# The norm behind two attention stages, done group by group inside the attention's loop

## The chip, the cores and the metric

One core of one Trainium2 chip runs the whole program. The time is that of the device, in microseconds (us), from the start of an execution to its end. The core has five engines with a queue of instructions each, which run in order and wait for each other by semaphores: PE multiplies matrices, DVE and POOL work on elements, ACT evaluates functions, and SP starts transfers. SBUF holds the data, and PE writes into eight banks of PSUM.

## What is computed

Four layers run over x of shape (16, 256, 128), that is 4096 tokens of 128 values. Each layer has an attention-like part and a feed-forward part, and each of the eight parts looks like this:

```python
h = _layernorm(x, axis=-1) * (1 + ca) + sa
x = x + ga * attention(h)
h = _layernorm(x, axis=-1) * (1 + cb) + sb
x = x + gb * feed_forward(h)
```

The scales and shifts differ for each of the 16 batches of 256 tokens. Two of the attention parts have 16 heads of 8 values: that of layer 1, which is causal and goes through a latent of 32, and that of layer 3, which sees all of a batch's 256 tokens. Behind the first comes a soft mixture of experts, whose first step needs the normed tokens of all batches. Behind the second comes a choice of 512 tokens for each of 8 experts. It begins with the logits: the normed tokens times an 8-column matrix.

## The kernel before

x stays in SBUF as `k.X`, 32 tiles of 128 tokens. The normed, scaled and shifted h of a part stands in `k.HT`, turned so that its columns are tokens. A norm over all tokens (`layernorm_dve`, `layernorm_pe`, `layernorm_act`, L283 to L317) goes as follows. The variance of each tile is known from `stats` (L179, L181). DVE adds eps to all 32 variances, ACT takes the square root, DVE the reciprocal. Then for each tile DVE subtracts and scales (L294) into one of eight tiles `xn`, PE turns that into a quarter of a PSUM bank (L170), and ACT scales and shifts a batch's two tiles into `k.HT` (L317). In the last layer PE also computes the logits there (`logits_pe`, L1188), a few for every two tiles turned.

A second form works on a group of four tiles, 512 tokens or two batches, numbered 0 to 7: `group_root_dve` (L328) takes the root by three rounds of Newton's method, all on DVE and on 4 columns: 6 instructions in the first of its three parts, 4 in the second and 4 in the third, each waiting for the one before. `group_rows_dve` (L348) norms two tiles, `group_turn_pe` turns four, `group_out_act` (L365) writes the two batches. The norm ahead of each attention with 16 heads has this form already. Its groups 0 to 6 run inside the loop of the part before, and its last one, group 7, runs in slots 0 to 5 of the attention (steps `norm` and `ht`).

An attention with 16 heads (`heads_*`) is a list of steps that `heads_steps` writes out by slot, and each engine walks the whole list in order. There are 4 slots for each batch, 64 in all, and a few behind them. In a slot, `far` (PE, then ACT's exponential L1085) makes the scores of one slot, `near0` and `near1` (PE L883, then DVE L1003 and L1005 or L1008) find the maximum of a slot six ahead, and `pv` applies the weights of the slot before. The rest of a batch's work is spread by the slot number modulo 4, as `misc` has it: `q0` and `k0` in 0, `out`, `nat0` and `nat1` in 1, `mb` at the start of 2 and `mt`, `q1` and `k1` behind it, `v`, `back` and `x` in 3. `x` adds the result of a batch to `k.X`, 11 slots after the batch's first, and `stats` of that batch come a slot later. All small products share two banks, `a.side`, in turn: a use waits until the use before last has been read out (`heads_room`).

The program does the parts one after the other: `heads_*`, then `layernorm_*`, then the mixture (`soft_*`) or the choice (`gate_rows_pe`, `pick_*`).

Of the kernel before, what the change touches and what calls it, by code (L numbers as in the profile page):

```python
# [324 lines left out]
ROOTS = 3  # L325
# [30 lines left out]
def group_turn_pe(k, n, e, B, bank):  # L356
    for j in range(4):
        e.wait_ge(*k.s_xn(32 * n.no + 4 * B + j + 1))
        transpose(k, e, bank[:, 128 * j:128 * j + 128], n.xn[(4 * B + j) % 8]).then_inc(k.s_turned.sem, 1)
# [384 lines left out]
AHEAD_UNITS = 9  # L744


def heads_plan(k, l, no, causal, w, t_w, norm):
    a = K()
    a.l, a.no, a.causal, a.w, a.t_w, a.norm = l, no, causal, w, t_w, norm
    a.scale = 8 ** -0.5  # L750
    a.slots = 4 * NB
    a.w1 = 128 if causal else 256
    a.qT, a.kT = ([k.QK[:, 512 * i + 2560 * j:512 * i + 2560 * j + 512] for i in range(5)] for j in range(2))
    R, G = Region(k.T, TW), Region(k.gbbc, 2048)
    a.PT = R.many(2, 2048)
    a.oT, a.va = R.many(2, 1024), R.many(2, 1024)
    a.whole, a.mb, a.junk = R.many(2, 512), R.many(2, 256), [k.W2[:, 384 * i:384 * i + 384] for i in range(2)]
    a.mx, a.rin = R.many(2, 32), R.many(2, 16)
    a.pick, a.hb = R.get(256).bitcast(BF16), R.get(16).bitcast(BF16)
    a.wo, a.msel, a.rows = R.get(128), R.get(4), [R.many(2, 32) for _ in range(2)]  # L760
    a.bga = R.get(16)
    a.mT = [R.get(128).bitcast(BF16) for _ in range(2)]
    a.lats, a.oN, a.oc, a.yT = G.many(2, 256), G.many(2, 256), G.many(2, 256), G.many(2, 256)
    a.near, a.side, a.far = k.bank[0:2], k.bank[2:4], k.bank[4:8]
    a.steps = list(heads_steps(a))
    a.ahead = a.steps.index(("far", 0))
    a.uses = {}
    for step in a.steps:
        if step[0] not in ("far", "near0", "near1", "mb", "norm", "stats"):
            a.uses[step] = len(a.uses)  # L770
    n = len(a.uses)
    a.s = sems(k, "h", side=n, free0=(n + 1) // 2, free1=n // 2, far=4 * a.slots, near=4 * a.slots, max=4 * a.slots,
               exp=4 * a.slots, kept=a.slots, high=0 if causal else 4 * NB, low=4 * NB, mb=NB, ready=5)
    return a
# [7 lines left out]
def heads_rest(a):  # L782
    return a.steps[a.ahead:]


def heads_steps(a):


    misc = {0: (("q0", 8), ("k0", 8), ("stats", -12)), 1: (("out", -9), ("nat0", -5), ("nat1", -5)),
            2: (("mt", 2), ("q1", 6), ("k1", 6)), 3: (("v", 1), ("back", -7), ("x", -11), ("lat", 9))}  # L790
    yield "wo", 0
    for s in range(-9, a.slots + 9):
        if 0 <= s < a.slots:
            yield "far", s
        if s % 4 == 2 and 0 <= s + 2 < a.slots:
            yield "mb", (s + 2) // 4
        if 0 <= s + 6 < a.slots:
            yield "near0", s + 6
        if 0 <= s - 1 < a.slots:
            yield "pv", s - 1  # L800
        if 0 <= s < ROOTS + 2:
            yield "norm", s
        if s == ROOTS + 2:
            yield "ht", 7
        for i, (step, ahead) in enumerate(misc[s % 4]):
            if i == 1 and 0 <= s + 6 < a.slots:
                yield "near1", s + 6
            n = (s + ahead) // 4
            if 0 <= n < NB and (step != "lat" or a.causal):
                yield step, n  # L810


def head(c, g):
# [24 lines left out]
    return a.s["free1" if u % 2 else "free0"](u // 2 + 1)  # L838


def heads_pe(k, a, e, steps):
    s, w = a.s, a.w
    e.wait_ge(*a.t_w)
    for step, n in steps:
        if step in ("mb", "stats", "norm"):
            pass
        elif step == "ht":
            group_turn_pe(k, a.norm, e, n, heads_room(a, e, step, n))
            e.wait_ge(*k.s_turned(32 * a.no + 4 * n + 4))
            e.nop().then_inc(s["side"].sem, 1)  # L850
        elif step == "far":
            b, c = divmod(n, 4)
            q, kk, m, at = *heads_part(a, n), a.mT[b % 2], 256 * (c % 2)
# [18 lines left out]
        elif step in ("near0", "near1"):  # L872
            b, c = divmod(n, 4)
# [107 lines left out]
def heads_dve(k, a, e, steps):  # L981
# [3 lines left out]
    for step, n in steps:  # L985
        if step == "norm":
# [83 lines left out]
def heads_act(k, a, e, steps):  # L1070
# [1 line left out]
    filled = lambda step, n: s["side"](a.uses[step, n] + 1)  # L1072
    e.wait_ge(*a.t_w)
    for step, n in steps:
        if step == "ht":
            o, free = heads_filled(a, e, step, n)
            group_out_act(k, a.norm, e, n, o)
            e.wait_ge(*k.s_h(16 * a.no + 2 * n + 2))
            e.nop().then_inc(free.sem, 1)
        elif step == "far":  # L1080
            if n >= 2:
# [1715 lines left out]
def program(nc, dram, out, phases):  # L2797
    ctx = ExitStack()
    with ctx:
# [5 lines left out]
        ln = [None] * 8  # L2805
        ln[0] = layernorm_plan(k, 0, 0, 0, r(), 0)
        a0 = attention_plan(k, 0, 0, views(k.W1, L0A), d["l0a"])
        r1 = r()
        g0 = gate_rows_plan(k, 0, 0)
        ln[1] = layernorm_plan(k, 0, 1, 1, r1, 1)  # L2810
        f0 = fold_plan(k, 0, 1, g0, d["l0f"], r1)
        ln[2] = f0.norm = layernorm_plan(k, 1, 0, 2, f0.big)
        a1 = f0.after = heads_plan(k, 1, 2, True, dict(sm, wo=sm["wproj"], bo=sm["bproj"]), d["sm"], ln[2])
        a1.begin, a1.emptied, a1.unread = f0.s["lifted"](60), (f0.s["sum"](8), k.s_h(16 * 2 + 14)), ()
        ln[3] = layernorm_plan(k, 1, 1, 3, r(), 2)
        f1 = soft_plan(k, 3, d["l1f"], d["l0f"])
        ln[4] = layernorm_plan(k, 2, 0, 4, r(), 3)
        f2 = rwkv_plan(k, 4, sm, d["sm"], d["l1f"], d["l0f"])
        r1 = r()
        g2 = gate_rows_plan(k, 2, 1)  # L2820
        ln[5] = layernorm_plan(k, 2, 1, 5, r1, 4)
        f3 = moe_plan(k, 2, 5, g2, d["l2f"], r1)
        ln[6] = f3.norm = layernorm_plan(k, 3, 0, 6, f3.big)
        a3 = f3.after = heads_plan(k, 3, 6, False, dict(sm, wo=sm["o3"], bo=sm["bo3"]), d["sm"], ln[6])
        a3.begin, a3.emptied = f3.s["lifted"](116), (f3.s["sum"](8 * 17), k.s_h(16 * 6 + 14))
        a3.unread, a3.added = range(28, 32), f3.s["tox"](8)
        r1 = r()
        g3 = gate_rows_plan(k, 3, 2)
        ln[7] = layernorm_plan(k, 3, 1, 7, r1, 5)
        f4 = pick_plan(k, 3, 7, g3, d["l3f"], r1)  # L2830
        done_by = lambda sub: k.s_aggr(32 * (sub + 1))

        block = ctx.enter_context(nc.Block())
# [32 lines left out]
        @block.tensor  # L2866
        def _(e):
            modulation_pe(k, mod, e)
            layernorm_pe(k, ln[0], e)
            attention_pe(k, a0, e)  # L2870
            layernorm_pe(k, ln[1], e, logits_pe(k, f0, e))
            gate_rows_pe(k, g0, e)
            fold_pe(k, f0, e)
            heads_pe(k, a1, e, heads_rest(a1))
            layernorm_pe(k, ln[3], e)
            soft_pe(k, f1, e)
            layernorm_pe(k, ln[4], e)
            rwkv_pe(k, f2, e)
            layernorm_pe(k, ln[5], e, logits_pe(k, f3, e))
            gate_rows_pe(k, g2, e)  # L2880
            moe_pe(k, f3, e)
            heads_pe(k, a3, e, heads_rest(a3))
            layernorm_pe(k, ln[7], e, logits_pe(k, f4, e))
            gate_rows_pe(k, g3, e)
            pick_pe(k, f4, e)

        @block.vector
        def _(e):
            modulation_dve(k, mod, e)
            e.wait_ge(*d["x"])  # L2890
            for i in range(NT):
                stats(k, e, i)
            layernorm_dve(k, ln[0], e, k.s_mod(1))
            attention_dve(k, a0, e)
            layernorm_dve(k, ln[1], e)
            fold_dve(k, f0, e)
            heads_dve(k, a1, e, heads_rest(a1))
            layernorm_dve(k, ln[3], e)
            soft_dve(k, f1, e)
            layernorm_dve(k, ln[4], e)  # L2900
            rwkv_dve(k, f2, e)
            layernorm_dve(k, ln[5], e)
            moe_dve(k, f3, e)
            heads_dve(k, a3, e, heads_rest(a3))
            layernorm_dve(k, ln[7], e)
            pick_dve(k, f4, e)

        @block.scalar
        def _(e):
            modulation_act(k, mod, e)  # L2910
            layernorm_act(k, ln[0], e)
            attention_act(k, a0, e)
            layernorm_act(k, ln[1], e)
            fold_act(k, f0, e)
            heads_act(k, a1, e, heads_rest(a1))
            layernorm_act(k, ln[3], e)
            soft_act(k, f1, e)
            layernorm_act(k, ln[4], e)
            rwkv_act(k, f2, e)
            layernorm_act(k, ln[5], e)  # L2920
            moe_act(k, f3, e)
            heads_act(k, a3, e, heads_rest(a3))
            layernorm_act(k, ln[7], e)
            pick_act(k, f4, e)

        @block.gpsimd
# [156 lines left out]
```

## Time and profile before

| what | us |
|---|---|
| median of 3 runs | 4153.87 |
| lowest and highest of them | 4150.37, 4159.74 |
| the profiled execution | 4153.31 |
| its span in the trace | 4151.6 |
| PE, DVE, ACT, POOL busy | 3767.8, 3238.5, 2228.8, 1281.9 |

The trace gives for each instruction when it ran, and how long its engine sat idle before it and for whom. "Busy" is an average over the whole span; the two stages that the change touches lie at about 1866 to 2174 us (layer 1) and 3567 to 3912 us (layer 3). A granted clock (PEclk) of 1.00 is the 2.4 GHz level of PE, 0.50 the 1.2 GHz level.

### The profile page before, as it was taken

The page shows a single profiled execution, that of the slowest core. Times are in us where ns is not written, and L with a number is a line of the kernel's source. Part 1 is how long each engine was busy: PE and PEld are TensorE (multiplying, and loading weights), DVE is VectorE, ACT ScalarE, POOL GpSimd, SP SyncE. Part 2 cuts the span into 40 slices and gives each one's busy share as a digit, 9 for nine tenths or more (in the row PEclk, how much of TensorE's full clock was granted, in tenths as well). Part 3 has the DMA queues.
Part 4 walks back from the last instruction along what each step waited for, and adds up shares of the span by engine and source line. Part 5 has one row for each costly group of instructions (what it writes and reads, how often), then busy time and mean ns, then how long its engine had stood idle before and what let it go on. Part 6 is the DMA issues. An engine that isn't in the chain of part 4 may idle for free.

```text
span 4151.6 us, 77967 instructions
## 1 busy us (share of the span) xinstructions
PE 3767.8 (91%) x25067; PEld 2529.9 (61%) x25067; DVE 3238.5 (78%) x11883; ACT 2228.8 (54%) x6889; POOL 1281.9 (31%) x1084
## 2 busy tenths in 40 slices
PE   6999999999999998989989978989978999899735
PEld 5777777777777776666654434335555666555533
DVE  6888888888888886667769986777886778788561
ACT  4877777778777774226764433332223222577401
POOL 1333333333333331014537865540000000222007
PEclk9999999999999998998999999999977999899757
DMA  2000000000000001211000000000000000000203
GB/s 121 2 1 2 1 2 1 2 1 2 2 2 2 2 1 51 88 55 62 2 2 0 0 10 1 1 0 1 1 1 32 1 1 1 31 2 2 62 9 52
DMA packets 30835, 63.57 MB, mean 15 GB/s; under 512 B 3424, under 2 KB 19808, under 8 KB 29152
## 3 DMA queue, kind: packets, MB, share of 16 engines
q1 hardware_dynamic: 24288, 52.29, 3.6%
q0 software_dynamic: 6144, 6.30, 0.9%
q8 instruction: 205, 3.36, 0.3%
q14 instruction: 198, 1.62, 0.1%
HBM read 49.93 MB, written 8.65 MB: 14 GB/s over the span
## 4 chain that ended last, share of the span: by engine, by line
PE 71%; DVE 15%; issue 7%; ACT 5%; POOL 2%; DMA 1%; DVEq 0%; POOLq 0%; ACTq 0%; SPq 0%
PE ps L462 9%; PE ps L501 9%; PE ps L170 8%; PE ps L443 6%; PE ps L486 5%; PE ps L1573 3%; PE ps L1544 3%; PE ps L1542 3%; DVE gbbc L2189 2%; PE ps L2137 2%; PE ps L2150 2%; PE ps L919 2%; DVE gbbc L2178 2%; DVE gbbc L2184 2%; PE ps L897 2%
## 5 line engine op out<-in xcount | busy, mean ns | idle before, releaser
L587 DVE CUSTOM_DVE_ANT_0 T<-ps,C 128x128 f32<-128x128 f32 x2048 | 451.4, 286 | 1.9
L734 POOL TENSOR_TENSOR W<-W,T 128x512 f32<-128x512 f32 x256 | 260.7, 1039 | 525.3 <-DVE T L623 525.3
L681 ACT ACTIVATE W<-T 128x128 f32<-128x128 f32 x1024 | 396.0, 391 | 46.0 <-DVE T L608 46.0
L734 POOL TENSOR_TENSOR T<-T 128x512 f32<-128x512 f32 x256 | 260.8, 1039 | 484.9 <-DVE T L623 484.9
L462 PE MATMUL ps<-T 64*128 64x128 f32 (+1 forms) x4096 | 405.5, 338 | 4.3 <-DVE T L587 4.3
L462 PEld LDWEIGHTS ps<-T 64*128 64x128 f32 x4096 | 344.6, 187 | 85.6 <-issue 64.5
L681 ACT ACTIVATE T<-T 128x128 f32<-128x128 f32 x1024 | 396.2, 391 | 0.0
L501 PE MATMUL ps<-W,gbbc 128*64 128x256 f32 x3072 | 388.1, 388 | 3.1 <-ACT T L698 3.1
L598 DVE COPY_PREDICATED W<-gbbc,ps 128x512 f32<-128x512 int32 x512 | 342.7, 721 | 38.0 <-PE ps L170 38.0
L170 PE MATMUL ps<-C,T 128*128 128x128 f32 (+1 forms) x1617 | 264.1, 301 | 63.4 <-DVE T L294 33.5
L170 PEld LDWEIGHTS ps<-C,T 128*128 128x128 f32 (+1 forms) x1617 | 196.0, 149 | 141.1 <-issue 45.5
L443 PE MATMUL ps<-HT,W 128*128 128x256 f32 x1024 | 278.2, 394 | 2.1 <-ACT HT L317 1.1
L1146 POOL TENSOR_TENSOR QK<-T,QK 128x512 fp32r<-128x512 f32 x128 | 162.7, 1280 | 378.3 <-ACT T L1106 260.4
L1085 ACT ACTIVATE T<-ps 128x384 f32<-128x384 f32 (+1 forms) x512 | 236.0, 550 | 71.2 <-PE ps L870 71.1
L501 PEld LDWEIGHTS ps<-W,gbbc 128*64 128x64 f32 x3072 | 197.9, 136 | 108.8 <-ACT T L698 4.2
L486 PE MATMUL ps<-T,W 128*128 128x256 f32 x1024 | 242.3, 379 | 0.8 <-ACT T L698 0.8
L575 DVE COPY_PREDICATED ps<-C,ps 128x256 f32<-128x256 int32 x512 | 195.6, 422 | 56.0 <-PE ps L462 55.8
L690 ACT ACTIVATE W<-ps 128x512 f32<-128x512 f32 x256 | 152.8, 597 | 139.0 <-PE ps L170 134.8
L1594 ACT ACTIVATE T<-ps,W 128x512 f32<-128x512 f32 x128 | 87.8, 687 | 240.2 <-PE ps L1542 240.1
L170 PE MATMUL ps<-C,W 128*128 128x128 f32 x1232 | 174.5, 284 | 45.8 <-DVE W L2762 21.2
L443 PEld LDWEIGHTS ps<-HT,W 128*128 128x128 f32 x1024 | 174.7, 190 | 64.6 <-issue 47.5
L170 PEld LDWEIGHTS ps<-C,W 128*128 128x128 f32 x1232 | 143.4, 145 | 103.1 <-issue 37.5
(403 smaller groups left out, 8801.2 us busy)
## 6 DMA issues: line engine op xcount, KB each, us to landing
T<-crow_dram SPq DMA_DIRECT2D x128, 128.0 KB, 3.0
W<-in_l1f_dram SPq DMA_DIRECT2D x1, 6152.0 KB, 18.3
W<-in_l0a_dram SPq DMA_DIRECT2D x1, 5172.5 KB, 24.7
W<-in_l2f_dram SPq DMA_DIRECT2D x1, 3160.0 KB, 11.2
W<-in_l3f_dram SPq DMA_DIRECT2D x1, 3076.0 KB, 10.9
W<-in_sm_dram SPq DMA_DIRECT2D x1, 2729.0 KB, 10.3
W<-in_l0f_dram SPq DMA_DIRECT2D x1, 2256.0 KB, 29.4
X<-in_x_dram SPq DMA_DIRECT2D x1, 2048.0 KB, 12.9
```

The costliest lines, as they stand in the source:

```text
L170: return e.transpose(out, in_, k.C["ident"])
L443: done(e.matmul(a.side[:, 256 * c:256 * c + 256], w["wq"][:, 512 * g + 128 * (2 * j + c):512 * g + 128 * (2 * j + c) + 128], x, start=True ...
L462: m = e.matmul(o, q[r, 256 * c + 128 * qt:256 * c + 128 * qt + 128], kt[r, k0:k0 + w_], start=True, stop=True)
L486: done(e.matmul(a.acc[:, 0:256], w["wo"][:, (g * a.CH + c) * 128:(g * a.CH + c + 1) * 128], a.oT[n % 2][:, 256 * c:256 * c + 256], start=( ...
L501: done(e.matmul(a.Ob[64 * r:64 * r + 64, at:at + 256], v[:, 128 * tile + g0:128 * tile + g0 + 64], x[:, r], start=(c != 1), stop=(c != 0)) ...
L575: e.copy_predicated(tiles[:, 0], old.bitcast(I32), tiles[:, 1]).then_inc(s["merged"].sem, 1)
L587: done(e.tensor_tensor_reduce(sm[:, at:at + 128], src, m, 1.0, -3.0e38, ALU.add, ALU.max, mx[:, col:col + 1]), s["masked"], x == (3 if ban ...
L598: e.copy_predicated(a.PT[t % 2][:, 512 * j:512 * j + 512].rearrange("p (h w) -> p h w", h=4), is_.unsqueeze(1).broadcast_to([P, 4, 128]).b ...
L681: done(e.activation(a.Pr[i % 4][:, at:at + w_], a.Sm[i % 2][:, at:at + w_], ACT.Exp, bias=a.ngs[i % 4][:, c:c + 1], scale=a.scale, accum_o ...
L734: e.tensor_tensor(pr, pr, a.rins[i % 4][:, c:c + 4].unsqueeze(2).broadcast_to([P, 4, 128]), ALU.mult).then_inc(s["norm"].sem, 1)
L1085: e.activation(a.PT[n % 2][:, 512 * g:512 * g + 256 + a.w1], a.far[g][:, 0:256 + a.w1], ACT.Exp, bias=0.0, scale=a.scale).then_inc(s["exp" ...
L1146: e.tensor_tensor(dst, a.whole[m % 2], dst.bitcast(F32), ALU.subtract).then_inc(s["low"].sem, 1)
```

## The change

Both norms behind the attentions with 16 heads take the form by groups, and their steps stand in the attention's own list. With B the number of a group, its three root parts stand at the end of slots 17, 18 and 19 + 8B, its two pairs of rows at the end of slots 20 and 21 + 8B, and the turning and writing, `ht2`, at the end of slot 22 + 8B. `ht2` takes a turn in the two side banks like the other small products. Slots now run to 78. So the `layernorm_*` calls behind the attentions are gone, with their root on ACT. In layer 3 the logits of batches 0 to 13 stand in slot 73, and those of batches 14 and 15 at the end. The tiles `xn` of these norms move into a free part of `k.W2`.

```diff
@@ heads_plan
-        if step[0] not in ("far", "near0", "near1", "mb", "norm", "stats"):
+        if step[0] not in ("far", "near0", "near1", "mb", "norm", "stats", "root", "rows", "logits"):
             a.uses[step] = len(a.uses)
@@ heads_steps
-    for s in range(-9, a.slots + 9):
+    for s in range(-9, a.slots + 15):
...
             n = (s + ahead) // 4
             if 0 <= n < NB and (step != "lat" or a.causal):
                 yield step, n
+        B, part = divmod(s - 17, 8)
+        if 0 <= B < 8:
+            if part < ROOTS:
+                yield "root", 8 * B + part
+            elif part < ROOTS + 2:
+                yield "rows", 8 * B + part - ROOTS
+            elif part == ROOTS + 2:
+                yield "ht2", B
+        if s == a.slots + 9:
+            yield "logits", 0
+    yield "logits", 1
@@ heads_pe
-        elif step == "ht":
-            group_turn_pe(k, a.norm, e, n, heads_room(a, e, step, n))
-            e.wait_ge(*k.s_turned(32 * a.no + 4 * n + 4))
+        elif step in ("ht", "ht2"):
+            norm = a.norm if step == "ht" else a.next
+            group_turn_pe(k, norm, e, n, heads_room(a, e, step, n))
+            e.wait_ge(*k.s_turned(32 * norm.no + 4 * n + 4))
             e.nop().then_inc(s["side"].sem, 1)
+        elif step == "logits":
+            for b in (range(14, 16) if n else range(14)) if logits is not None else ():
+                logits(b)
@@ heads_dve
+        elif step == "root":
+            group_root_dve(k, a.next, e, *divmod(n, 8))
+        elif step == "rows":
+            group_rows_dve(k, a.next, e, n // 8, ((0, 1), (2, 3))[n % 8])
@@ heads_act
-        if step == "ht":
+        if step in ("ht", "ht2"):
+            norm = a.norm if step == "ht" else a.next
             o, free = heads_filled(a, e, step, n)
-            group_out_act(k, a.norm, e, n, o)
-            e.wait_ge(*k.s_h(16 * a.no + 2 * n + 2))
+            group_out_act(k, norm, e, n, o)
+            e.wait_ge(*k.s_h(16 * norm.no + 2 * n + 2))
             e.nop().then_inc(free.sem, 1)
@@ program, PE's queue (DVE's and ACT's lose the same layernorm calls)
             heads_pe(k, a1, e, heads_rest(a1))
-            layernorm_pe(k, ln[3], e)
             soft_pe(k, f1, e)
...
-            heads_pe(k, a3, e, heads_rest(a3))
-            layernorm_pe(k, ln[7], e, logits_pe(k, f4, e))
+            heads_pe(k, a3, e, heads_rest(a3), logits_pe(k, f4, e))
             gate_rows_pe(k, g3, e)
```

On DVE, in layer 1 at the end of slot 17 (a slot that is 1 modulo 8), the changed kernel has these rows between `nat1` (L1074, L1076) and `mb` (L1044 to L1048):

```order
L1074 RECIPROCAL T<-ps 128x16
L1076 TENSOR_TENSOR gbbc<-ps,T 128x128
L334 TENSOR_SCALAR rs<-MV 128x4
L336 TENSOR_SCALAR rs<-rs 128x4
L338 TENSOR_TENSOR rs<-rs 128x4
L340 TENSOR_TENSOR rs<-rs 128x4
L342 TENSOR_SCALAR rs<-rs 128x4
L344 TENSOR_TENSOR rs<-rs 128x4
L1044 CAST T<-T 128x32
L1046 CAST T<-T 128x8x4
L1048 TENSOR_TENSOR T<-T 128x8x4
```

Before, `mb` followed `nat1` at once, and the six rows L334 to L344 were not there.

On PE, in the same stage at the end of a slot that is 6 modulo 8, the changed kernel has the four turns of `ht2` between `q1` and `k1` (L936) and the next slot's `far` (L883, L887), `near0` (L900) and `pv` (L914):

```order
L936 MATMUL ps<-gbbc,W 128x256 x4
L170 MATMUL ps<-C,W 128x128 x4
L883 MATMUL ps<-QK 128x256 x4
L887 MATMUL ps<-T 128x256 x4
```

Before, `far` followed `k1` at once. The nop that PE carries out behind the turns, when they are done, is not among the rows.

On PE, at the end of layer 3's attention, the changed kernel has `out` of batch 15 (L969), then `ht2` of group 6, the last `x`, the logits of 14 batches (L1210), `ht2` of group 7, and the last logits ahead of the gate's rows (L257):

```order
L969 MATMUL ps<-gbbc,T 128x256
L170 MATMUL ps<-C,W 128x128 x4
L170 MATMUL ps<-C,gbbc 128x128 x2
L1210 MATMUL ps<-W,HT 128x8 x28
L170 MATMUL ps<-C,W 128x128 x4
L1210 MATMUL ps<-W,HT 128x8 x4
L257 MATMUL ps<-C,modT 128x128 x16
```

Before, 32 turns with 32 logits among them stood between the last `x` and L257, and nothing stood between `out` and the last `x`.

## Rows read from the trace of the kernel before

**Rows 1.** Windows: length, then PE, PEld, DVE, ACT, POOL busy, then PEclk.
```profile
2066.00:2083.80 17.80, 16.91 (x200) 11.11 (x198) 13.66 (x83) 12.75 (x29) 9.44 (x9) 1.00 0.01 2
3812.19:3851.07 38.88, 36.66 (x395) 23.00 (x394) 33.74 (x77) 28.48 (x56) 10.13 (x9) 1.00 0.01 2
...
2160.00:2165.00 5.00, 1.50 (x6) 0.74 (x6) 3.53 (x15) 2.08 (x3) 0.00 (x0) 0.68 0.00 0
...
3894.00:3902.00 8.00, 8.00 (x43) 7.92 (x43) 5.58 (x21) 4.16 (x9) 0.00 (x0) 0.50 0.60 172
```

**Rows 2.** Chain of waits, layer 1: start, length, engine and line.
```profile
2091.53 0.68 PE ps L913 x4
...
2103.31 0.18 DVE T L1023
...
2105.11 0.49 PE ps L883 x3
```

**Rows 3.** Chain of waits, layer 3.
```profile
3827.14 1.20 DVE T L1008 x2
...
3831.11 0.61 ACT T L1106
```

**Rows 4.** Timeline of DVE, group 7 of the norm ahead of layer 3's attention.
```profile
3571.94 0.17 DVE L334 TENSOR_SCALAR rs<-MV 128x4 f32<-128x4 f32 x1
...
3573.14 0.69 DVE L1015 TENSOR_TENSOR T<-ps,W 128x512 f32<-128x512 f32 x1
...
3578.15 0.22 DVE L338 TENSOR_TENSOR rs<-rs 128x4 f32<-128x4 f32 x1
...
3579.00 1.29 DVE L1008 TENSOR_REDUCE T<-ps 128x2 f32<-128x512 f32 x2
...
3595.58 0.59 DVE L352 TENSOR_SCALAR W<-X,MV,rs 128x128 f32<-128x128 f32 x2
```

**Rows 5.** Timeline of DVE in both loops: in brackets the idle time before.
```profile
2090.60 0.29 DVE L1003 CUSTOM_DVE_ANT_0 W<-ps,C 128x128 f32<-128x128 f32 x1 [1.69 <-PE ps L883]
...
3834.55 1.29 DVE L1008 TENSOR_REDUCE T<-ps 128x2 f32<-128x512 f32 x2 [0.73 <-PE ps L883]
```

**Rows 6.** Timeline of ACT, layer 3: exponentials of a batch's first slots, and L365.
```profile
3593.01 2.06 ACT L1085 ACTIVATE T<-ps 128x512 f32<-128x512 f32 x4 [0.78 <-PE ps L870]
...
3602.02 1.04 ACT L365 ACTIVATE HT<-ps,modT 128x256 f32<-128x256 f32 x2
...
3614.00 2.06 ACT L1085 ACTIVATE T<-ps 128x512 f32<-128x512 f32 x4 [0.51 <-PE ps L870]
...
3815.00 2.06 ACT L1085 ACTIVATE T<-ps 128x512 f32<-128x512 f32 x4 [0.51 <-PE ps L870]
...
3834.44 2.06 ACT L1085 ACTIVATE T<-ps 128x512 f32<-128x512 f32 x4 [0.51 <-PE ps L870]
```

**Rows 7.** Timelines of POOL and of DVE at one place in layer 1's attention.
```profile
1888.86 1.10 POOL L1150 TENSOR_SCALAR_AFFINE_SELECT T<-T 128x1024 f32<-128x1024 f32 x1 [0.24 <-ACT T L1085]
...
1889.25 1.04 DVE L352 TENSOR_SCALAR W<-X,MV,rs 128x128 f32<-128x128 f32 x2
```

**Rows 8.** Chain of waits, end of layer 1's attention and of the norm behind it.
```profile
2158.31 0.27 DVE T L1053
...
2161.83 0.43 DVE X L1063
...
2173.88 3.73 PE ps L170 x32
```

**Rows 9.** Timeline of ACT at the same place.
```profile
2161.25 1.28 ACT L313 ACT_TABLE_LOAD   x1
```

**Rows 10.** Chain of waits, end of layer 3's attention and of the norm behind it.
```profile
3889.12 0.43 DVE X L1063
...
3907.47 4.07 PE ps L1188 x20
3911.54 5.99 PE ps L257 x32
```

More of the change, by code:

```diff
@@ L744, with heads_plan @@
 AHEAD_UNITS = 9
-def heads_plan(k, l, no, causal, w, t_w, norm):
+def heads_plan(k, l, no, causal, w, t_w, norm, after):
     a = K()
-    a.l, a.no, a.causal, a.w, a.t_w, a.norm = l, no, causal, w, t_w, norm
+    a.l, a.no, a.causal, a.w, a.t_w, a.norm, a.next = l, no, causal, w, t_w, norm, after
     a.scale = 8 ** -0.5
@@ L838, in heads_taken, with heads_pe @@
     return a.s["free1" if u % 2 else "free0"](u // 2 + 1)
-def heads_pe(k, a, e, steps):
+def heads_pe(k, a, e, steps, logits=None):
     s, w = a.s, a.w
@@ L844, in heads_pe @@
     for step, n in steps:
-        if step in ("mb", "stats", "norm"):
+        if step in ("mb", "stats", "norm", "root", "rows"):
             pass
-        elif step == "ht":
-            group_turn_pe(k, a.norm, e, n, heads_room(a, e, step, n))
-            e.wait_ge(*k.s_turned(32 * a.no + 4 * n + 4))
+        elif step in ("ht", "ht2"):
+            norm = a.norm if step == "ht" else a.next
+            group_turn_pe(k, norm, e, n, heads_room(a, e, step, n))
+            e.wait_ge(*k.s_turned(32 * norm.no + 4 * n + 4))
             e.nop().then_inc(s["side"].sem, 1)
+        elif step == "logits":
+            for b in (range(14, 16) if n else range(14)) if logits is not None else ():
+                logits(b)
         elif step == "far":
@@ L2807, in program @@
         a0 = attention_plan(k, 0, 0, views(k.W1, L0A), d["l0a"])
+        spare = lambda: Region(k.W2[:, 768:], 1024)
         r1 = r()
@@ L2812, in program @@
         ln[2] = f0.norm = layernorm_plan(k, 1, 0, 2, f0.big)
-        a1 = f0.after = heads_plan(k, 1, 2, True, dict(sm, wo=sm["wproj"], bo=sm["bproj"]), d["sm"], ln[2])
+        ln[3] = layernorm_plan(k, 1, 1, 3, spare())
+        a1 = f0.after = heads_plan(k, 1, 2, True, dict(sm, wo=sm["wproj"], bo=sm["bproj"]), d["sm"], ln[2],
+                                  ln[3])
         a1.begin, a1.emptied, a1.unread = f0.s["lifted"](60), (f0.s["sum"](8), k.s_h(16 * 2 + 14)), ()
-        ln[3] = layernorm_plan(k, 1, 1, 3, r(), 2)
         f1 = soft_plan(k, 3, d["l1f"], d["l0f"])
-        ln[4] = layernorm_plan(k, 2, 0, 4, r(), 3)
+        ln[4] = layernorm_plan(k, 2, 0, 4, r(), 2)
         f2 = rwkv_plan(k, 4, sm, d["sm"], d["l1f"], d["l0f"])
@@ L2820, in program @@
         g2 = gate_rows_plan(k, 2, 1)
-        ln[5] = layernorm_plan(k, 2, 1, 5, r1, 4)
+        ln[5] = layernorm_plan(k, 2, 1, 5, r1, 3)
         f3 = moe_plan(k, 2, 5, g2, d["l2f"], r1)
         ln[6] = f3.norm = layernorm_plan(k, 3, 0, 6, f3.big)
-        a3 = f3.after = heads_plan(k, 3, 6, False, dict(sm, wo=sm["o3"], bo=sm["bo3"]), d["sm"], ln[6])
+        ln[7] = layernorm_plan(k, 3, 1, 7, spare())
+        a3 = f3.after = heads_plan(k, 3, 6, False, dict(sm, wo=sm["o3"], bo=sm["bo3"]), d["sm"], ln[6],
+                                  ln[7])
         a3.begin, a3.emptied = f3.s["lifted"](116), (f3.s["sum"](8 * 17), k.s_h(16 * 6 + 14))
         a3.unread, a3.added = range(28, 32), f3.s["tox"](8)
-        r1 = r()
         g3 = gate_rows_plan(k, 3, 2)
-        ln[7] = layernorm_plan(k, 3, 1, 7, r1, 5)
-        f4 = pick_plan(k, 3, 7, g3, d["l3f"], r1)
+        f4 = pick_plan(k, 3, 7, g3, d["l3f"], r())
         done_by = lambda sub: k.s_aggr(32 * (sub + 1))
@@ L2897, in _ @@
             heads_dve(k, a1, e, heads_rest(a1))
-            layernorm_dve(k, ln[3], e)
             soft_dve(k, f1, e)
@@ L2904, in _ @@
             heads_dve(k, a3, e, heads_rest(a3))
-            layernorm_dve(k, ln[7], e)
             pick_dve(k, f4, e)
@@ L2915, in _ @@
             heads_act(k, a1, e, heads_rest(a1))
-            layernorm_act(k, ln[3], e)
             soft_act(k, f1, e)
@@ L2922, in _ @@
             heads_act(k, a3, e, heads_rest(a3))
-            layernorm_act(k, ln[7], e)
             pick_act(k, f4, e)
```

## The prediction

> **What bounds the kernel now.** I looked at the windows of the two attentions first, for how full each engine is. In layer 1 a batch takes 17.80 us, PE works in 16.91 of them and DVE in 13.66; in layer 3 two batches take 38.88 us, with PE at 36.66 and DVE at 33.74 [rows 1]. So DVE is free for 4.1 us per batch in layer 1 and for (38.88 - 33.74) / 2 = 2.6 us in layer 3. That looks like room. But all queues run in order, so next I read the chain of waits, to see whose work has no slack. In layer 1 the chain lies on DVE from `near1` through `nat0`, `nat1` and `mb` (L1023 at 2103.31) to the next `near0`, and PE's `near1` (L883, 2105.11) waits for it; later in the batch it runs through ACT's `q1` and `k1` to PE's `v` (L913 at 2091.53) [rows 2]. In layer 3 it runs through DVE's `near1` (L1008 at 3827.14) and then through ACT's `k1` (L1106 at 3831.11) [rows 3]. DVE's free time lies elsewhere: 1.69 us behind slot 2 modulo 4 in layer 1, 0.73 us behind slot 3 modulo 4 in layer 3 [rows 5].
>
> Last the two ends. In layer 1 the last `x` is added at 2161.83 and the mixture's first turns start at 2173.88, 12.05 us later [rows 8]. In layer 3 the last `x` stands at 3889.12 and the gate's rows at 3911.54, 22.42 us later [rows 10]. In that end PE is busy in 8.00 of 8.00 us at a granted clock of 0.50 [rows 1], and the last 20 logit matmuls take 4.07 us, 0.204 us each [rows 10]. A logit is carried out as two matmuls, so there are 64 of these for 32 tiles.
>
> **What a group adds in the loop.** Prices come from group 7 of the norm ahead [rows 4]. The first root part runs from 3571.94 to 3573.14, 1.20 us. The second runs from 3578.15 to 3579.00, 0.85 us; the third is as long. A pair of rows takes 0.59 us. L365 for two batches takes 1.04 us on ACT [rows 6]. Group by group, at each place:
> - First root part, behind `nat1` and ahead of `mb`: nothing covers it. In layer 1 `mb` and PE's `near1` are on the chain [rows 2], so 1.20 us. In layer 3 PE and DVE are level there, within about 0.15 us, so 1.05 us. PE, and then everybody, waits.
> - Second and third part: in layer 1 the 1.69 us of free time covers the second [rows 5]; the third meets a similar gap. In layer 3 the third falls into 0.73 us [rows 5] and the second ahead of a stretch in which the chain is on ACT. I take 0. If that cover is gone, each costs 0.85 us.
> - First pair of rows, behind `stats`: it delays `near0`, and PE's `near1` is only partly waiting. 0.3 us in layer 1, 0.2 us in layer 3.
> - Second pair, behind `nat1` like the first root part: 0.6 us in layer 1, 0.45 in layer 3.
> - `ht2`, behind `k1`: on ACT it stands between `k1` and the next exponentials, 1.04 us and some 0.15 for the wait for its own writes. On PE four turns and the wait for their end come ahead of `far`. `v` now takes the side bank that `ht2` held, so PE waits at `v` for ACT's `ht2`; queued behind are `near1`, `back` and `x`. Both ways it is about 1.2 us, on the chain in both layers [rows 2, 3].
>
> The sum is 1.20 + 0.3 + 0.6 + 1.2 = 3.3 us in layer 1 and 1.05 + 0.2 + 0.45 + 1.2 = 2.9 us in layer 3. Five groups (0 to 4) lie in the full loop. Group 5 meets slots without `near0` and `near1`, where DVE is half idle; I give it 1.5 us, mostly `ht2`. Layer 1: 5 x 3.3 + 1.5 = 18. Layer 3: 5 x 2.9 + 1.5 = 16. Together 34 us.
>
> The trace has one place that bounds this. In layer 3, slots 4 to 8 hold one pair of rows and one `ht` and last from 3593.01 to 3614.00, 20.99 us; the same slots of a later batch last from 3815.00 to 3834.44, 19.44 us [rows 6]. So this half of a group, at kinder places, costs 1.55 us. That is my lower bound for a whole group: ten of them 16 us, and nothing for group 5. The upper bound has the first part at 1.20, each pair of rows at 1.04 and `ht2` at 1.2: 4.5 us, so 45 + 3 = 48 us.
>
> Why 1.04: beside a POOL instruction that began at 1888.86 two rows took 1.04 us and not 0.59 [rows 7]. The Trainium skill says the same ("GPSIMD Engine Reference", Specifications): POOL shares its SBUF interfaces with VectorE, and they contend in VectorE's two-port mode or with two SBUF inputs. It speaks against this change, since the new work on DVE is all of that kind. By the row without POOL the sum is 34 us; by this rule it would be up to 10 x 2 x 0.45 = 9 us more, were POOL always busy. This trace agrees at that place.
>
> **The ends.** Group 6 stands between `nat1` and the last `x`, and `x` waits on PE behind `ht2`. Layer 1: `nat1` begins at 2158.31 [rows 8] and is done some 0.6 us later. Then DVE has 1.20 + 0.85 + 0.85 for the root, 0.4 and 0.9 for `x` and `stats` of batch 14, 1.2 for the rows; turning and the wait add 0.5 and `x`'s own turns 0.4. The last `x` is added at about 2165.1, 3.3 us late. Behind it come 1.4 us for `stats`, 2.9 for group 7's root, 1.2 for its rows, 0.4 for the turns and 1.1 for ACT: 2172.1, against 2173.88. That gains 1.8 us. But PE has hardly worked since 2160 (1.50 of 5.00 us, clock down to 0.68 [rows 1]), so the mixture's first 32 turns, 3.73 us at full clock [rows 8], begin at the half clock; I give back 1.8 us. Layer 1's end: 0.
>
> Layer 3: the last `x` is again 3.2 us late, at 3892.3. Then PE has the logits of 14 batches, 56 matmuls at 0.204 us: 11.4 us, to 3903.7. DVE's 1.4 + 2.9 + 1.2 us lie beside them and are hidden; without that cover they would cost 5.5 us. Behind the logits come four turns at the half clock (1.1 us), ACT (1.0) and eight matmuls (1.6): 3907.5 against 3911.54. That gains 4.0 us. PE was the bound of this end before, and of the 64 logit matmuls none has gone beside other PE work; only 28 turns have left it.
>
> The square root on ACT goes too, with its table load of 1.28 us. The load ran at 2161.25, while ACT waited for the last `x` [rows 9], so it gives 0. The Trainium skill ("ScalarE: Activation LUTs", What ACT_TABLE_LOAD costs) puts a switch of tables at about 2.66 us, drain included. By it, four switches on the path would be worth 10.6 us; by the row they are hidden.
>
> **Sum**, against the profiled execution, which lies 0.6 us under the median: 4153.3 + 34 - 4.0 = 4183.3 us.
>
> **Rivals.**
> 1. The free time on DVE absorbs the groups, and the time isn't slower. The free share of [rows 1] and the gaps of [rows 5] speak for it, the zero slack in [rows 2, 3] and the 1.55 us of [rows 6] against. At no cost per group the ends alone count, with the 1.8 us if the mixture starts warm: 4153.3 - 4.0 = 4149, or 4147. It decides at about 1.0 us per group: 12 x 1.0 - 4 is the 0.2% (8.3 us) that a measurement of this kernel can tell from no change. 0.12.
> 2. PE's stalls let its clock fall inside the loops. It stands at 1.00 in both now [rows 1], with PE at 95% and 94%, and falls to 0.68 at the end, where PE waits. In the changed loop PE waits for some 1.2 us twice per group. If half of the groups lost 2.5 us more each, the time would be 4183 + 15 = 4198. 0.15.
> 3. The logits run at full clock, because PE comes to them straight from the loop's last turns. 64 x 0.1 us are gained: 4177. Against it: the clock stayed at 0.50 for 8 us of PE without a gap [rows 1]. 0.1.
> 4. The forecast, a group at 2 to 4 us: 0.63.
>
> **Range.** Low: 4153.3 + 16 - 5.8 = 4163.5. High: 4153.3 + 48 - 2 = 4199, which takes in rival 2. Below 4164 lies most of rival 1, above 4199 part of rival 2. Faster by over 0.2% needs rival 1 and rival 3 together: 0.04. Within 0.2%: the rest of rival 1 and a little of the low bound, 0.10. Slower: 0.86.
>
> **What the changed profile would show.** Two batches of layer 1 take about 38.9 us in place of 35.6, two of layer 3 about 41.8 in place of 38.9. DVE's L334 to L344 follow `nat1` without a gap and PE's `near1` waits behind them. ACT's exponentials behind `ht2` come about 1.2 us late, and PE waits at `v` for L365. The logits of 14 batches run in one piece for 11 to 12 us at clock 0.50, and the gate's rows start about 18.4 us behind the time at which the last `x` would have come. What would make it wrong: chains that have more slack than one profiled batch shows, or a clock that falls in the loops.

## The result, and the profile after

The changed kernel takes 4265.5 us (median of 4 runs, 4262.4 to 4273.3) against 4152.9 for the kernel before: a ratio of 1.027, with a 95% interval of 1.025 to 1.029. I forecast 4183 us and at most 4199. Slower was right; the size was not, +112 us where I had +29. The profiled execution has a span of 4263.2 us, against 4151.6. (The ratios here are estimated from all runs on one chip and differ a little from the quotients of the medians.)

Where did it go? Four events cut a span into stages: the first exponential of an attention, its last `x`, the mixture's first turns (layer 1) or the gate's rows (layer 3), and the first exponential of layer 3. In us:

| kernel | layer 1: first exponential to last `x` | to the mixture | to layer 3's first exponential | there: to last `x` | to the gate's rows | rest |
|---|---|---|---|---|---|---|
| before | 293.5 | 12.05 | 1394.6 | 320.6 | 22.3 | 240.2 |
| changed | 396.4 | 7.03 | 1397.8 | 340.1 | 15.1 | 240.5 |

So 103 of the 112 us lie in one loop, that of layer 1. Windows of the changed kernel (columns as in [rows 1], the granted clock of PE is the third number from the end):

```profile
1866.00:2262.00 396.00, 369.11 (x3086) 234.77 (x3085) 241.04 (x1353) 204.36 (x444) 141.48 (x120) 0.68 0.04 17
1966.00:1970.00 4.00, 3.87 (x56) 2.52 (x50) 3.56 (x22) 2.62 (x7) 2.38 (x2) 1.00 0.01 2
1970.00:1974.00 4.00, 1.66 (x19) 0.95 (x12) 3.68 (x18) 1.34 (x4) 1.10 (x1) 1.00 0.00 0
1974.00:1978.00 4.00, 4.00 (x26) 2.79 (x25) 1.52 (x12) 1.96 (x4) 1.06 (x1) 0.52 0.00 0
1994.00:1998.00 4.00, 4.00 (x28) 2.51 (x21) 2.31 (x14) 1.57 (x4) 1.94 (x2) 0.50 0.02 4
2002.00:2006.00 4.00, 3.12 (x21) 2.23 (x20) 1.46 (x9) 2.72 (x6) 1.71 (x2) 1.00 0.00 0
3667.00:4007.00 340.00, 306.69 (x3064) 188.09 (x3065) 278.75 (x718) 227.21 (x431) 72.89 (x59) 0.93 0.03 11
```

The first row is layer 1's whole stage, at a mean clock of 0.68. The same stage of the kernel before, and its layer 3:

```profile
1868.00:2162.00 294.00, 275.37 (x3058) 179.21 (x3056) 211.54 (x1228) 196.16 (x432) 141.20 (x120) 0.93 0.06 23
3568.00:3889.00 321.00, 301.16 (x3037) 184.45 (x3037) 256.13 (x592) 220.74 (x419) 72.91 (x59) 0.93 0.03 11
```

PE has the 28 turns of seven groups more, and is 94 us longer busy. Layer 3's stage (last row) has 0.93, as it had before. The rows between show one fall: from 1970 to 1974 PE works only 1.66 of 4.00 us, then the clock is 0.52 and 0.50, and although PE is then busy in 4.00 of 4.00 us it is back at 1.00 only from 2002 on, 28 us later. The timelines show what PE waited for, first DVE's:

```profile
1969.21 0.29 DVE L1076 TENSOR_TENSOR gbbc<-ps,T 128x128 f32<-128x128 f32 x1
1969.42 0.16 DVE L334 TENSOR_SCALAR rs<-MV 128x4 f32<-128x4 f32 x1
...
1970.61 0.18 DVE L1044 CAST T<-T 128x32 bf16<-128x32 f32 x1
1970.82 0.18 DVE L1046 CAST T<-T 128x32 f32<-128x32 bf16 x1
1971.04 1.13 DVE L1048 TENSOR_TENSOR T<-T 128x32 f32<-128x32 f32 x1
```

Then POOL's and PE's at the same place:

```profile
1971.03 1.10 POOL L1172 TENSOR_SCALAR_AFFINE_SELECT T<-T 128x1024 f32<-128x1024 f32 x1 [2.37 <-ACT T L1107]
```

```profile
1972.32 0.41 PE L170 MATMUL ps<-C,T 128*128 128x128 f32 x2 [2.02 <-DVE T L1048]
```

The first root part takes its 1.20 us behind `nat1`, as forecast. But it moves `mb` so that its last instruction, L1048, starts 0.01 us behind POOL's select, and it takes 1.13 us instead of 0.19. PE's `mt` waits 2.02 us. That happens at 1971, 2021, 2071 and 2119, and the clock falls at each of the four. The fifth time, at 2178, L1048 is not held (0.19 us), and the clock is low already.

The two ends came as forecast. PE at the end of layer 3, and the last `x` on DVE, which answer to [rows 10]:

```profile
4005.43 1.15 PE L170 MATMUL ps<-C,W 128*128 128x128 f32 x4 [2.63 <-DVE W L352]
4006.89 0.66 PE L170 MATMUL ps<-C,gbbc 128*128 128x128 f32 x2 [0.30 <-PE ps L170]
4007.34 11.96 PE L1210 MATMUL ps<-W,HT 128*128 128x8 f32 x56
4019.15 1.09 PE L170 MATMUL ps<-C,W 128*128 128x128 f32 x4
4020.99 1.87 PE L1210 MATMUL ps<-W,HT 128*128 128x8 f32 x8 [0.75 <-ACT HT L365]
4022.71 5.22 PE L257 MATMUL ps<-C,modT 128*128 128x128 f32 x32
```

```profile
4007.58 0.42 DVE L1084 TENSOR_TENSOR X<-X,ps 128x256 f32<-128x256 f32 x1 [1.53 <-PE ps L170]
```

### The profile page after: what moved, and what is told of

It is laid out like the page before. It is cut to its first block, busy times and chain, and to the rows that moved or that the text cites. A ratio compares the mean times of both kernels' runs of the same rounds, so it can differ in the third digit from the quotient of the medians.

```text
span 4263.2 us, 78227 instructions
## 1 busy us (share of the span) xinstructions
PE 3856.3 (90%) x25067; PEld 2582.4 (61%) x25067; DVE 3277.6 (77%) x12103; ACT 2226.0 (52%) x6883; POOL 1281.1 (30%) x1084
## 4 chain that ended last, share of the span: by engine, by line
PE 72%; DVE 17%; issue 4%; ACT 4%; POOL 2%; DMA 1%; DVEq 0%; POOLq 0%; ACTq 0%; SPq 0%; PEldq 0%
PE ps L462 9%; PE ps L501 9%; PE ps L170 8%; PE ps L443 6%; PE ps L486 5%; PE ps L936 3%; PE ps L1595 3%; PE ps L1566 3%; PE ps L1564 3%; DVE gbbc L2211 2%; PE ps L2172 2%; PE ps L2159 2%; PE ps L900 2%; PE ps L914 2%; DVE gbbc L2200 2%
## 5 line engine op out<-in xcount | busy, mean ns | idle before, releaser
L170 PE MATMUL ps<-C,T 128*128 128x128 f32 (+1 forms) x1553 | 248.5, 300 | 67.1 <-DVE T L294 28.1
L170 PE MATMUL ps<-C,W 128*128 128x128 f32 x1296 | 190.0, 290 | 56.3 <-DVE W L2784 21.2
L170 PEld LDWEIGHTS ps<-C,W 128*128 128x128 f32 x1296 | 154.1, 147 | 120.4 <-issue 49.3
```

Of the source, the lines that this page charges most:

```text
L170: return e.transpose(out, in_, k.C["ident"])
```

## The experiments

Theory A: stalls of PE in layer 1's loop make its granted clock fall, and the half clock costs most of the 112 us. Theory B, the rival: the added work and its waits cost it as such. Each version is compared with the kernel before on the same chip (4149 to 4153 us). Layer 3's stage is 320.6 us long before and 340.1 in the changed kernel; it is given below where it moved again.

**One layer alone.** Layer 3 (or layer 1) gets its `layernorm_*` behind the attention back:

```diff
+        ln[3] = layernorm_plan(k, 1, 1, 3, r(), 2)          # layer 3 only
-        if 0 <= B < 8:
+        if 0 <= B < 8 and a.next is not None:
```

> Only layer 1's attention does the norm behind it by groups; layer 3 is as before. Theory A (the loss is the granted clock of PE, which falls in layer 1's loop, where a stall of 2.02 us stands ahead of mt in every second batch): layer 3 began 99 us late in the changed kernel, so this version takes 4153 + 99 = 4252 us, 4240 to 4262. Theory B (each group costs its added work, and layer 3's dearer batches cost as much as layer 1's): half of the 112 us, about 4210.

> Only layer 3's attention does the norm behind it by groups; layer 1 is as before. Theory A: layer 3 lost 12 us in the changed kernel by the two traces (loop +14.8, end -7.3, the rest clock at its start), so 4165 us, 4160 to 4172, with PE's clock at 1.00 in nearly all of the loop. Theory B: about 4210.

Layer 1 alone: 4238.9 us (4224.3 to 4266.1), ratio 1.023 (1.019 to 1.028). Layer 3 alone: 4168.3 us, ratio 1.0044 (1.0027 to 1.0060). The loss lies in layer 1, as A has it; the first time lies 1 us under A's range, the second inside it. One kernel's runs being 42 us apart is new, and goes with the clock: the mean granted clock of the whole run was 0.920, 0.919, 0.911 and 0.907 at 4224.3, 4225.8, 4252.1 and 4266.1 us. By the table layer 3's net 12 us are 19.5 in its stage less 7.1 at its end; slots 0 to 16 took 85.6 us against 85.7, so the clock at its start had no part in them.

**PE kept at work in the stall.**

```diff
             o = heads_room(a, e, step, n)          # step mt
+            for i in range(16 if n % 2 and n > 3 else 0):
+                transpose(k, e, o[:, 128 * (i % 2):128 * (i % 2) + 128], k.C["ident"])
             e.wait_ge(*s["mb"](n + 1))
```

> The changed kernel, in which PE carries out 16 more turns of the identity into mt's own bank ahead of its wait for mb, in each odd batch from 5 on: some 1.9 us of needless PE work where it stalled for 2.02 us. No work on DVE or ACT changes. Theory A (clock): the clock stays at 1.00 in most of layer 1's loop, and most of the 75 us that slots 16 to 56 lost come back; some 3.3 us per group stay: about 4195 us, 4180 to 4215. Theory B (the added work and waits as such): nothing comes back, and 12 places with up to 1.9 us more on PE give 4265 to 4285.

4199.6 us, ratio 1.0118 (1.0095 to 1.0141): more work on PE, and 66 us less than the changed kernel. (Slots 16 to 56 had lost 81 us, 258.3 against 177.4, and not the 75 of the expectation.) The whole stage of layer 1:

```profile
1868.00:2193.00 325.00, 299.51 (x3181) 198.41 (x3180) 239.30 (x1354) 203.82 (x445) 141.32 (x120) 0.90 0.05 21
```

95 instructions more on PE than in the changed kernel, 70 us less busy time: that is the clock, 0.90 for 0.68. Theory B falls. The turns leave 0.64 us of each of five stalls, and behind each of these the clock still falls, for 3 us.

**Everything one slot later.** `divmod(s - 18, 8)` for `divmod(s - 17, 8)`.

> The changed kernel with all of a group's steps one slot later (root parts at the end of slots 18, 19 and 20 + 8B, pairs of rows 21 and 22, ht2 23), so that only one pair of rows, 0.59 us, stands between nat1 and mb, and no root part. The work is the same. Theory A (the stall ahead of mt makes the clock fall): the stall shrinks from 2.02 us to under 0.8, the clock stays up in most of layer 1's loop, and the time is 4180 to 4215 us. Theory B (the added work): 4255 to 4275, no difference.

4248.7 us, ratio 1.023 (1.021 to 1.026): neither theory's number. The stall at `mt` is gone, but the third root part now stands ahead of `near1`, and another instruction of POOL holds L342 of it. DVE of this version:

```profile
1971.08 0.16 DVE L340 TENSOR_TENSOR rs<-rs 128x4 f32<-128x4 f32 x1
1971.27 1.25 DVE L342 TENSOR_SCALAR rs<-rs 128x4 f32<-128x4 f32 x1
1972.55 0.16 DVE L344 TENSOR_TENSOR rs<-rs 128x4 f32<-128x4 f32 x1
```

Its PE, and a window of it:

```profile
1973.54 0.29 PE L900 MATMUL ps<-QK 32*128 32x128 f32 x1 [1.50 <-DVE T L1026]
```

```profile
2026.00:2138.00 112.00, 110.60 (x742) 70.29 (x742) 58.88 (x338) 49.12 (x106) 34.38 (x29) 0.50 0.01 1
```

PE stalls for 1.50 us three times. The clock falls at once behind the first two, for 3 and for 123 us, with PE busy in 110.60 of 112.00 us in the second fall; behind the third it falls only 6 us later, after one more stall of 0.64 us. My error was to take the stall ahead of `mt` for the only one that the groups can make. Layer 3 lost by the move too: its stage is 356.5 us long, with stalls of 2.26 to 2.67 us ahead of `near1`. This window also prices the low clock: inside it `ht2` is 60.55 us from the next (2031.33 to 2091.88), where two batches and a group take 38.4 at full clock (below). An us at half clock loses 0.37 us. Slots 0 to 16 agree, with the same instructions in both: 83.9 us with the clock low for 41 us in the kernel before, 78.4 with 26 us low in the version with layer 3 alone, so 0.38.

**The stall alone.** The kernel before, and needless instructions on 4 columns ahead of `mb`, in layer 1's odd batches from 5 on:

```diff
+            for i in range(6 if a.causal and n % 2 and n > 3 else 0):      # 2 in the other version
+                ...
             c_.then(e.tensor_copy(a.hb, a.mx[n % 2]))
```

> The kernel before, with nothing of the change, but with six needless instructions on 4 columns ahead of mb in layer 1's odd batches from 5 on (1.2 us of DVE each time, the length and place of the first root part), six times in all. Theory A (a PE stall of some 2 us at that place makes the clock fall): POOL's select holds the last of mb as well, PE stalls for 2 us, the clock falls for 18 us or more behind each, and the time grows by 40 to 90 us, to 4190 to 4240. Theory B (the stalls as such): 6 x 1.2 to 2.0 = 7 to 12 us, to 4157 to 4162.

> As the run before, with two needless instructions (0.4 us) in place of six. mb ends ahead of POOL's select by the trace of before, so that PE should stall for 0.4 to 0.6 us. Theory A, if it takes a long stall for the clock to fall: 4151 to 4156, clock at 1.00 as in the kernel before. Rival A2 (any stall at this place is enough, since PE has no slack there): the time of the run before, 4190 to 4240. Theory B: 6 x 0.4 = 2 us, which can't be told from A.

Six instructions: 4192.5 us, ratio 1.013 (1.010 to 1.016). Some 7 us of added time on DVE cost 44. Two instructions: 4154.2, ratio 1.0011 (0.9999 to 1.0023), no difference. DVE's L1034 in the first version is the last instruction of `mb`, and the profile has it both ways:

```profile
1962.04 1.13 DVE L1034 TENSOR_TENSOR T<-T 128x32 f32<-128x32 f32 x1
...
2052.18 0.19 DVE L1034 TENSOR_TENSOR T<-T 128x32 f32<-128x32 f32 x1
...
2125.77 0.19 DVE L1034 TENSOR_TENSOR T<-T 128x32 f32<-128x32 f32 x1
```

POOL's select beside it:

```profile
1962.03 1.10 POOL L1157 TENSOR_SCALAR_AFFINE_SELECT T<-T 128x1024 f32<-128x1024 f32 x1 [2.36 <-ACT T L1092]
...
2052.46 1.10 POOL L1157 TENSOR_SCALAR_AFFINE_SELECT T<-T 128x1024 f32<-128x1024 f32 x1 [2.65 <-ACT T L1092]
...
2125.77 1.16 POOL L1157 TENSOR_SCALAR_AFFINE_SELECT T<-T 128x1024 f32<-128x1024 f32 x1 [2.36 <-ACT T L1092]
```

Started 0.01 us behind the select, it is held; started 0.28 us ahead, it is not. At 2009.74, 2088.98 and 2125.77 both start in the same 0.01 us: DVE's isn't held, and POOL's takes 1.15 or 1.16 us. PE's stall is 2.01 us the first time, and 1.07 the next four times. Where the clock stayed up, 1.2 us of DVE's work lengthened two batches from 35.62 to 36.80 us, by 1.18, and 0.4 us by 0.39 (a stall of 0.27 or 0.28 us, five times): what I had counted. Where the clock fell, two batches took 7 to 12 us more.

**A shorter first part.** The root's first part keeps 2 of its 6 instructions; the second does two rounds.

```diff
-            group_root_dve(k, a.next, e, *divmod(n, 8))
+            group_root_dve(k, a.next, e, *divmod(n, 8), (0, 2, 1))   # rounds in each part
```

> The changed kernel; only the root is cut otherwise: the first part (slot 17 + 8B) keeps its two instructions on the variance, 0.4 us, the second takes two rounds of Newton's method (1.6 us, where DVE had 1.69 us free), the third one round. Same work in the same slots. Theory A: PE's stall ahead of mt is 0.4 to 0.8 us, the clock stays up in most of layer 1's loop, and the time is 4175 to 4210, unless POOL holds an instruction elsewhere and makes another stall over 1.5 us. Theory B (the added work): 4255 to 4275.

4217.9 us, ratio 1.0170 (1.0155 to 1.0186): 48 us come back without a single instruction less, though not as many as I expected. In layer 1's loop no stall reaches 0.9 us. One of 0.62 to 0.64 us is left behind the second pair of rows; the clock fell behind three of five such. Layer 3's stage grew from 340.1 to 354.3 us. There the two rounds of the second part run into POOL, in each of the five groups, and PE's `near1` waits:

```profile
3709.34 1.13 DVE L341 TENSOR_TENSOR rs<-rs 128x4 f32<-128x4 f32 x1
3710.50 1.19 DVE L343 TENSOR_SCALAR rs<-rs 128x4 f32<-128x4 f32 x1
```

```profile
3712.76 0.35 PE L901 MATMUL ps<-QK 32*128 32x256 f32 x1 [2.56 <-DVE T L1030]
```

The clock falls behind each of these five stalls of 2.56 to 2.67 us too, but is back after 3 to 7 us.

**The same, with turns in what is left of the stalls.** 6 needless turns ahead of the wait for `mb`, from batch 5 on.

> The changed kernel with the short first root part, and with 6 needless turns on PE (some 0.7 us) ahead of its wait for mb in every batch from 5 on, where 0.4 to 0.64 us of stall are left. In the run with the short part alone the clock still fell twice in four times behind a stall of 0.62 to 0.64 us. Theory A (what is left over the added work is the clock's): the clock stays at 1.00 in layer 1's loop, a group costs the 2.7 to 3.1 us that it cost there at full clock, up to 0.7 more where the turns are too many, and the time is 4149 + 5 x 3 + 5 x 3.1 + 3 - 4 = 4179 us, 4170 to 4195. Theory B (the rest of the loss is work and waits): 4218 to 4230.

4192.7 us, ratio 1.0104 (1.0083 to 1.0125). Layer 1's stage, and two turnings of ACT in it:

```profile
1868.00:2173.00 305.00, 281.79 (x3152) 186.64 (x3150) 234.18 (x1351) 202.89 (x444) 141.31 (x120) 0.95 0.06 23
```

```profile
2017.74 0.58 ACT L366 ACTIVATE HT<-ps,modT 128x256 f32<-128x256 f32 x1
...
2056.11 0.58 ACT L366 ACTIVATE HT<-ps,modT 128x256 f32<-128x256 f32 x1
```

The clock is 1.00 from 1894 to the end of the loop, and a group costs 38.37 - 35.62 = 2.75 us. The stage is 305.1 us long with all of the change's work in it, against 396.4. My 4179 was too low because of layer 3, 353.6 us long where the sum counted 3 us a group, as in the changed kernel's 340.1. That isn't the turns, as the version before had 354.3 without one: it is the two-round second part, whose stalls of 2.55 to 2.71 us stand here as well.

**The groups in the tail.** A version meant to keep the ends' gain and leave the loops alone: groups 0 to 5 have one root over 24 columns from slot 57 on, rows and `ht2` in slots 60 to 67, and groups 6 and 7 come behind the last `x`. Then mended: root from slot 58, `ht2` in the banks of `near`. Then that in layer 3 alone, and once more in both.

```diff
+        if 58 <= s < 61:
+            yield "root", (0, 24, s - 58)
+        if 61 <= s < 67:
+            yield "rows", 8 * (s - 61)
+            yield "rows", 8 * (s - 61) + 1
+        if s in TURNS:
+            yield "ht2", TURNS.index(s)
+        if 66 <= s < 72:
+            yield "logits", range(2 * s - 132, 2 * s - 130)
...
+TURNS = (62, 64, 65, 66, 67, 69)
```

> A version that would keep the loops as before: groups 0 to 5 have one root over 24 columns in slots 57 to 59, their rows in slots 60 to 65 and ht2 in 62 to 67, where near0 and near1 have ended; groups 6 and 7 come behind the last x, with one root each; in layer 3 the logits of batches 0 to 11 stand in slots 69 and 71, beside DVE's end. Theory A (the loops lost the time, the ends gain): loops as before, layer 1's last x to the mixture about 10 us in place of 12.05, layer 3's last x to the gate's rows 10 to 13 in place of 22.4, the slots from 60 on up to 3 us longer in each layer: 4135 to 4148 against 4150. Theory B (any added work in the attention costs what it takes): no gain, 4150 to 4165.

> The version with the groups in the tail, mended: the root over 24 columns begins at the end of slot 58, behind the last mb (at slot 57 it made PE stall for 2.37 us in layer 1 and 1.33 us in layer 3), ht2 uses the two banks of near, so that PE waits neither for its own turns nor for the side banks, and the logits of batches 0 to 11 are spread over slots 66 to 71. Theory A: slots 56 to the last x some 1 to 3 us longer than before in each layer, the last x to the mixture 8 to 9 us in place of 12.05 and to the gate's rows 9 to 12 in place of 22.4: 4137 to 4146 against 4149. Rival: the tail is a chain over PE and ACT as tight as the loop, and the stages from 56 on grow by what the ends gain: 4147 to 4158.

> The version with the groups in the tail and the banks of near, in layer 3 only; layer 1 has its norm behind the attention, as in the kernel before. In the profile of the version in both layers, layer 1 gained nothing (slots 56 to the last x +2.0 us, the last x to the mixture -4.1, the mixture's first turns +2.2 at half clock), and layer 3 gained 12 us (the last x to the gate's rows 10.0 in place of 22.4), while its loop was 8 us longer than before with the same instructions in it. Theory C (that 8 us is the clock's scatter between executions, and the 12 us are real): 4137 to 4143 against 4149. Theory D (the 12 us are given back elsewhere in every execution): 4146 to 4152.

> The version with the groups in the tail of both layers once more, the same kernel, on the same chip as the run in layer 3 only: theory C 4137 to 4146, theory D 4146 to 4152, as the first time (4148.5 against 4152.5).

Ratios 1.0019 (1.0003 to 1.0035), 0.9995 (0.9982 to 1.0007), 0.9994 (0.9977 to 1.0011) and 0.9991 (0.9976 to 1.0006); medians 4161.6, 4148.5, 4148.7 and 4150.1. The first was worse for one more stall: its root part of slot 57 stood ahead of the last `mb`, PE waited 2.37 us, and the clock fell. None of the others can be told from the kernel before. Theory A missed both times (4161.6 against 4135 to 4148, then 4148.5 against 4137 to 4146), and its rivals' ranges held. The profiles of the last three show the gain at the end, from the last `x` to the gate's rows 10.0 us instead of 22.3. They also show where part of it goes: layer 3's stage up to the last `x` is 322 to 328 us long in them against 318 to 321 in the four kernels that leave it alone, and the middle of the program 1 to 3 us longer. The rest of the 12 us is not found; theory D fits better than C, but runs of one version are up to 26 us apart (4136.8 to 4163.0), and this stays open.

## Why the prediction was wrong

- **The first root part at `mb`, 1.20 us.** Right in place and size (1.18 where nothing else happened). What it lacked is POOL's hold of 0.94 us more, four times of five. I had such a row [rows 7] and charged it to the pairs of rows alone, as 0.45 us each; it struck the instruction that PE waits for. The kernel before holds a root instruction in the same way, at the head of layer 1's attention (DVE, then POOL):

```profile
1871.17 1.26 DVE L342 TENSOR_SCALAR rs<-rs 128x4 f32<-128x4 f32 x1
```

```profile
1871.15 1.26 POOL L1146 TENSOR_TENSOR QK<-T,QK 128x512 fp32r<-128x512 f32 x1
```

- **Parts two and three, both pairs, `ht2`.** The sum for a group in layer 1 was 3.3 us; measured at full clock 2.74 (short first part) and 2.75 (with turns). In layer 3 it was 2.9 us; two groups at full clock took 42.0 us against 38.9, so 3.1. But slots 16 to 56 took 217.3 us against 199.7, five times 3.5: the third group took 48.4 us. In that one POOL held L338 for 1.18 us and L344 for 1.26, and the clock was low for 10 us. With layer 3 changed alone, three of four turnings came 44.4 to 45.2 us behind the last. The stage as a whole grew by 19.5 us where 16 and 3.2 were forecast, and that is luck: its five full groups cost 17.6 us in place of 14.5, and what lies behind slot 56 cost 2.0 in place of 4.7.
- **Layer 1's end.** Forecast 7.0 us from the last `x` to the mixture, measured 7.03; half clock there 1.8, measured 6.02 - 3.73 = 2.3.
- **Layer 3's end.** Forecast 15.2 us from the last `x` (3892.3) to the gate's rows (3907.5), measured 15.13; 56 logits in 11.4 us, measured 11.96. The logits ran at the half clock (0.50 from 4008 to 4019): rival 3 is out.
- **The square root's table load** was given nothing, and no run isolates it; layer 1's end came out at the 7.0 us that were forecast without it.
- **The step that failed is the 18 us for layer 1**, and with it rival 2. The sum had the clock in the loop at nothing. Only rival 2 had it, with "half of the groups lost 2.5 us more each", 15 us in all. The mechanism was rival 2's; the size stood on no row. From one `ht2` to the next it measured 48 to 58 us where I had 38.9, in all 103 us for the stage, where 18 and 3.3 for the last `x` were forecast. Of these some 17 are work (305.1 us in the version with turns, at a clock of 0.95, against 287.9 with layer 1 unchanged, at 0.96). By mean clocks of 0.68 and 0.93, the changed stage spent 253 us at the low level and the stage before 41; 212 us more, at 0.37 us each, are 78. The last 8 us hold POOL's four holds of 0.94; the split is worked out, not tested. A row to size it by was there: [rows 1] has PE busy in 8.00 of 8.00 us at 0.50. I used it against rival 3 and not for the loop. The kernel before has a better one, in layer 1's own loop, where the clock stayed low from 1868 to 1909:

```profile
1880.00:1900.00 20.00, 20.00 (x132) 12.25 (x124) 10.37 (x57) 8.09 (x17) 6.35 (x6) 0.50 0.01 2
```

- **"It stands at 1.00 in both now"** holds for the two windows of [rows 1] and not for layer 3's loop. In slots 16 to 56 of the kernel before PE stalls ten times for 0.75 us, and behind four of these the clock is low for 3 us; the first of the four:

```profile
3662.77 0.66 PE L170 MATMUL ps<-C,T 128*128 128x128 f32 x4 [0.75 <-ACT gbbc L1117]
```

```profile
3663.70:3667.00 3.30, 3.30 (x38) 1.65 (x30) 2.29 (x8) 2.06 (x4) 0.00 (x0) 0.50 0.02 5
```

- **10.7 of the 103 us came before the change's first instruction.** Slots 0 to 16 are the same in both kernels, and to slot 6 the exponentials stand at the same distances to 0.01 us. Then the clock came back at some 1909 before and 1933 in the changed kernel, and between 1894 and 1931 in the profiles of the other versions, with the same instructions there. So this part isn't shown to come from the change.

The prediction named both causes. It gave the clock a fifth of its price, and looked for the hold in the wrong instructions.

## What to carry to other kernels

Where PE is 95% busy at the full clock, ask first what a new wait of PE's does to the granted clock. Price a fall by the stage's pace at 0.50 and by how long that same stage has stayed low with PE busy: tens of us in layer 1 here, 3 to 7 us in layer 3. Put small DVE work where PE doesn't wait behind it (0.4 us ahead of `mb` could not be told from nothing, 1.2 us in the same six places cost 44), and look at what POOL starts at that moment: 0.01 us decided whether a wait was 1.07 or 2.01 us. Look at every place that the work is moved to, in each stage that runs the code: the shorter first part helped layer 1 and cost layer 3 14 us. And a tail that looks 12 us shorter in one profile isn't a gain until the medians show it.

## What was not expected of the hardware

- In slots 16 to 58 of layer 1 the clock fell at all nine stalls of 2.01 to 2.37 us that PE made at full clock, and behind two of three of 1.50 us at once. It fell behind two of four of 1.07 us, not behind the one of 0.92, behind both of 0.74, and behind twelve of fifteen of 0.62 to 0.64. It fell behind none of eleven of 0.57 or 0.58 us and none of five of 0.27 or 0.28. Once low it stayed so from 3 us to 123 us.
- In the same slots of layer 3 fourteen stalls of 2.26 to 2.71 us (one slot later, short first part, with turns) all made it fall, but each time for 3 to 7 us only. What decides how long it stays low was not settled, and neither was why the two layers differ. The Trainium skill ("TensorE: Matmul & The Clock Gate", Part 1) has the full clock return soon once PE is busy again; these fourteen falls of layer 3 agree, and layer 1 doesn't, with PE busy in 110.60 of 112.00 us at 0.50.
- A TENSOR_SCALAR, TENSOR_TENSOR or CAST of DVE on SBUF data that takes 0.16 to 0.19 us alone is held when it starts 0.01 to 0.2 us behind one of POOL's, and ends with POOL's, 0.05 us later at most: 0.95 to 1.29 us after its start, 95 times of 95 in the two attentions of all profiles. It doesn't hold for each DVE instruction on SBUF data: beside POOL's at 1937.92 (1.28 us) in the kernel before, BATCH_NORM_STATS2 took its 0.29 us and BATCH_NORM_AGGREGATE its 0.18. The Trainium skill ("Trainium Architecture — The Big Picture", What this means for kernel authors) calls the port that the two share an exclusive lock and not a bandwidth split; the trace agrees for the held ones, with 1.13 us beside the select's 1.10.
